# Two of eight normaliser chunks of a linear-attention layer routed through memory instead of through TensorE

## Chip, cores and metric

The kernel runs on one core of one Trainium2 chip. The metric is the device time of one execution in microseconds (us), as the median of several executions. The engines are called by the names of the profile: PE is TensorE's matmul, PEld its weight load, DVE VectorE, ACT ScalarE, POOL GpSimd, and SP SyncE, which here only issues transfers and waits (SPq in the rows).

## What is computed

The input x has 8 batches of 512 tokens with 128 features. The first half is a linear attention with 16 heads of 64 features, the second a mixture of eight experts of which each token takes two. The part that matters, cut from the reference:

```python
q, k, v = split(x @ W_qkv)                       # 16 heads of 64
q, k = relu(q @ W_f + b_f), relu(k @ W_f + b_f)
kv = einsum('bhnd,bhne->bhde', k, v)
out = einsum('bhnd,bhde->bhne', q, kv)
normalizer = einsum('bhnd,bhd->bhn', q, k.sum(axis=2))
out = out / (normalizer[..., None] + 1e-06)
x = layernorm(x + out @ W_out + b_out)
# then: x = layernorm(x + mixture_of_experts(x))
```

There is one normaliser for each head and token. It has to divide all 64 features of its head.

## The kernel before

**Layout.** The 1024 query features lie as eight chunks of 128 partitions (`q_act[:, c, :]`, features down the partitions, the 512 tokens of a batch along a row). One chunk holds two heads, 64 partitions each. The reciprocal normalisers of a batch are a tile `rn[:, 1, :]` in which the two heads of chunk c stand on two neighbouring partitions of 128. To multiply chunk c by them, each of the two rows has to be brought to 64 partitions.

**How it is brought there before.** `r_hi`, `r_rest` (ACT, two ACTIVATEs, lines 838 and 839) and `r_hl` (DVE, line 1196) split the reciprocals into a high and a low part. For each chunk `spread_norm(c)` (line 566) is one PE matmul of a constant matrix of ones and zeros with `r_hl`, into one of the two halves of the PSUM tile `psG`. `normalise(c)` (line 1124) is the DVE product of `q_act` and `psG` into `qn`, and `output(c)` (line 575) the PE matmul of `qn` with the mixed values, summed over c in `psO`.

**Order of the work.** The orders of all engines are written out by hand, with semaphores between them. `attention(b)` is called for b = 0 to 8. Call b works on the keys and queries of batch b (`cur`, b below 8) and on the output of batch p = b - 1 (`prev`, b above 0). On PE a call is: `keys(0)`, `keys(1)`, `spread_norm(0)`; then for c = 0 to 7 `keys(c + 1)` (three matmuls, lines 465 to 467), `spread_norm(c + 1)`, `turn_keys(c)` (four transposes, line 554) and `output(c - 1)`; then `output(7)`, the eight `queries`, the logits of batch p, the normaliser sums (`norms`, line 597), the Gram matrices (`gram`, lines 465 to 467) and `mix` (line 622). In call 8 only `spread_norm` and `output` are left.

**The loop over c on the other engines.** ACT evicts each key chunk (`key`, into `kT`) and splits its transpose (`key_hi`, into `k_hi`). DVE does, for each c, `normalise(c)`, `key_lo(c - 1)` (line 893, into `k_lo`) and, for odd c, a row sum over two chunks (line 1136). `turn_keys(c)` waits for the eviction of chunk c and for `key_lo(c - 2)`; `output(c)` waits for `normalise(c)`; `spread_norm(c)` waits for `normalise(c - 2)`. In call 7 the DVE also works out a table of expert blocks in five parts (`early_table`), one in each of the steps c = 1 to 5. In calls 1 to 7 one or two expert weights are split by ACT and DVE as well (`SPLIT_AT`), and SP stores each and loads the next (lines 330 to 334).

**Where the reciprocals come from.** Late in call b the DVE adds the epsilon to the sums (line 1187) and takes two reciprocals of half a batch each (line 1191), after which the count of `n_step` is 3 (b + 1). `spread_norm(0)` of call b + 1 is the first that needs them.

**SP's queue before.** After the loads of the start, SP goes through the eight experts (wait for the split, store, load), then waits for the last batch's tokens and loads the second expert layer's weights (line 337), and later feeds the expert stage, which takes the time from some 303 us on.

Of the kernel before, what the change touches and what calls it, by code (L numbers as in the profile page):

```python
# [19 lines left out]
ALU = mybir.AluOpType  # L20
ACT = mybir.ActivationFunctionType
AX_X = mybir.AxisListType.X
F32 = mybir.dt.float32
# [6 lines left out]
P = 128  # L30
D = 128
B, S = 8, 512
N = B * S
TILES = S // P
H, DH = 16, 64
HD = H * DH
CH = HD // P
E, F = 8, 512
# [7 lines left out]
EARLY = -(-(SAFE * S * TOPK - E * (BLK - 1)) // BLK)  # L46
LATE = NBLK - EARLY
ERAS = (4, SAFE, B - 1, B)
# [9 lines left out]
CHAIN_AT = {37: ((0, 4),), 40: ((4, 6), (6, 7))}  # L58
NORM_AT = {38: 0}
PAIRED = 8  # L60
ROW = D + 4
XS_ROWS = E * REGION + BLK
NOWHERE = E * REGION
# [7 lines left out]
SPLIT_AT = {1: ((0, 2), (1, 5)), **{b: ((b, 3),) for b in range(2, B)}}  # L71
# [10 lines left out]
QUAD = 32  # L82
# [32 lines left out]
def program(nc, x, xT, wqkvT, wf, bf, wout, bout, gwT, w12, consts, out):  # L115
    ctx = ExitStack()
    with ctx:
        def sb(name, shape, dt=F32):
            return ctx.enter_context(nc.sbuf_tensor(name, shape, dt))

        def pb(name, shape, dt=F32):
            return ctx.enter_context(nc.psum_tensor(name, shape, dt))

        def sem(name):
            return ctx.enter_context(nc.semaphore(name))


        wb = nc.dram_tensor("expert_weights", [E, P, W_ROW], F32, kind="Internal").ap()
        xs = nc.dram_tensor("expert_rows", [XS_ROWS, ROW], F32, kind="Internal").ap()
        ys = nc.dram_tensor("expert_results", [TOPK * N, D], F32, kind="Internal").ap()  # L130


# [2 lines left out]
        def con(name, rows=P):  # L135
# [14 lines left out]
        q_act = sb("q_act", [P, CH, S])  # L150
        gm = sb("gm", [P, HD])
        mixed = sb("mixed", [P, CH, D])
        kT = sb("kT", [P, KT_SLOTS, S])
        ksum = sb("ksum", [P, CH])
        qn = sb("qn", [P, 4, S])
        rows_2 = [sb(f"rows{i}", [P, TILES, TOPK, ROW]) for i in range(2)]
        zeros = sb("zeros", [P, BLK // P, ROW])
        warm = sb("warm", [P, 2])
# [6 lines left out]
        tri_b = sb("tri_b", [P, P], BF16)  # L165
        ksd = sb("ksd", [P, CH, QUAD])
        rn = sb("rn", [P, 2, S])
        r_hi, r_rest = sb("r_hi", [P, S], F32R), sb("r_rest", [P, S])
        spread = sb("spread", [P, CH, P], F32R)
        r_hl = sb("r_hl", [P, S], F32R)  # L170
# [25 lines left out]
        at_row = sb("at_row", [1, len(ERAS) * E])  # L196
        jump = sb("jump", [1, len(ERAS) * E])
        endi = sb("endi", [1, E], I32)
        past = [sb(f"past{i}", [1, LATE * len(ERAS) * E]) for i in range(2)]
        tab = sb("tab", [1, 3, NBLK])  # L200
        tabi = sb("tabi", [1, 2, NBLK], I32)

# [3 lines left out]
        woutd = x1[:, 0:2 * CH, :].rearrange("p (c a) d -> p c a d", a=2)  # L206
        zT = qn[:, 3, :]
        kT_space = kT[:, :, :].rearrange("p c s -> p (c s)")
        rn_space = rn[:, :, :].rearrange("p a s -> p (a s)")
        qn_space = qn[:, :, :].rearrange("p a s -> p (a s)")  # L210
        hT = [q_space[:, v * FC * BLK:(v + 1) * FC * BLK].rearrange("p (c s) -> p c s", c=FC) for v in range(2)]
        yrow = [q_space[:, 2 * FC * BLK + 2 * u * D:2 * FC * BLK + 2 * (u + 1) * D].rearrange("p (c d) -> p c d", d=D) for u in range(SLOTS)]
        xrow = [space[:, 2 * u * ROW:2 * (u + 1) * ROW].rearrange("p (c d) -> p c d", d=ROW)
                for space, fit in ((kT_space, 7), (rn_space, ROW_SLOTS - 7)) for u in range(fit)]
# [10 lines left out]
        psG = pb("psG", [P, 2, 512])  # L225
# [10 lines left out]
        def bank_of(n):  # L236
            return n % 2 if n >= PAIRED else 0

        def before(n):
            return n if n <= PAIRED else n - 1  # L240

# [11 lines left out]
        ksum_done, ks_done, n_pe, n_step, qn_done, o_pe, zT_done = (  # L253
            sem(n) for n in ("ksum_done", "ks_done", "n_pe", "n_step", "qn_done", "o_pe", "zT_done"))
# [9 lines left out]
        w1_out = [sem(f"w1_out{i}") for i in range(2)]  # L264
        wb_in, w2_in = sem("wb_in"), sem("w2_in")
        in_xr0, in_fold_q, in_fold_v, tab_step = (sem(n) for n in ("in_xr0", "in_fold_q", "in_fold_v", "tab_step"))
        r_h, r_l, bc_pe, in_spread, spread_ready = (sem(n) for n in ("r_h", "r_l", "bc_pe", "in_spread", "spread_ready"))
        warmed, ends, padded, filled_rows = sem("warmed"), sem("ends"), sem("padded"), sem("filled_rows")
        scattered_2 = [sem(f"scattered_{i}") for i in range(2)]
# [6 lines left out]
        N_STEPS, LN_STEPS, ST_STEPS, ROUTE_STEPS = 3, 12, 2 * TILES, 22  # L276
# [26 lines left out]
        def _(sp):  # L303
# [19 lines left out]
            def load_w1(ex):  # L323
                sp.dma_start(w1_raw[ex % 2], w12[ex, :, 0:F]).then_inc(in_w1[ex % 2], 16)
# [2 lines left out]
            sp.dma_start(wb[:, :, 2 * F + FC:], w12[:, :, F + FC + FC * D:]).then_inc(wb_in, 16)  # L327
            load_w1(0)
            load_w1(1)
            for ex in range(E):  # L330
                sp.wait_ge(w1_l, ex + 1)
                sp.dma_start(wb[ex, :, 0:2 * F], w1_split[ex % 2].bitcast(F32)).then_inc(w1_out[ex % 2], 16)
                if ex + 2 < E:
                    load_w1(ex + 2)
            sp.wait_ge(x_l, B)
            sp.wait_ge(x_h, B)
            sp.dma_start(w2_all.rearrange("p (e n) -> p e n", e=E), w12[:, :, F + FC:F + FC + FC * D].rearrange("e p n -> p e n")).then_inc(w2_in, 16)
# [122 lines left out]
        def _(pe):  # L460
# [25 lines left out]
            def gate_mean():  # L486

                pe.wait_ge(in_c, 16)
                pe.wait_ge(in_small, 32)
                mm(psS[:, 0:E], con("ones"), gw[:, :], start=True, stop=True).then_inc(mean_pe, 1)  # L490
# [35 lines left out]
            def attention(b):  # L526
                cur, prev = b < B, 1 <= b <= B
                p = b - 1

                def keys(c):  # L530
                    if c == 0:
                        pe.wait_ge(xT_l, b + 1)
                    if c >= 2:
                        pe.wait_ge(kT_done, CH * b + c - 1)
                    if b == 0 and c % 4 == 0:
                        pe.wait_ge(fold_lo, 1 + c // 4)
                    at = slice(c * P, (c + 1) * P)
                    three(bankA[c % 2], wk_hi[:, at], wk_lo[:, at], xT_hi[:, :], xT_lo[:, :]).then_inc(kT_pe, 1)

                def turn_keys(c):  # L540
                    pe.wait_ge(kT_done, CH * b + c + 1)
                    if c == 0 and prev:
                        pe.wait_ge(m_first, b)
                    if c == 0 and b == 0:
                        pe.wait_ge(in_ident, 16)
                    if c == 1 and prev:
                        pe.wait_ge(m_second, b)
                    if c == 1 and b == 0:
                        pe.wait_ge(fold_lo, 2)
                    if c >= 2:  # L550
                        pe.wait_ge(k_l, CH * b + c - 1)
                    for t in range(TILES):
                        at = slice(t * P, (t + 1) * P)
                        last = pe.transpose(bankA[2 + c % 2][:, at], kT[:, (CH * b + c) % KT_SLOTS, at], con("ident"))  # L554
                    last.then_inc(kr_pe, 1)

                def spread_norm(c):

                    if c == 0:
                        pe.wait_ge(r_l, p + 1)  # L560
                        pe.wait_ge(spread_ready, 1)
                    if c < 2:
                        pe.wait_ge(g_done, 2 * (p + 1))
                    else:
                        pe.wait_ge(qn_done, CH * p + c - 1)
                    mm(psG[:, c % 2, :], spread[:, c, :], r_hl[:, :], start=True, stop=True).then_inc(bc_pe, 1)  # L566
# [64 lines left out]
                for c in range(CH):  # L631
                    if cur and c and c + 1 < CH:
                        keys(c + 1)
                    if prev and c + 1 < CH:
                        spread_norm(c + 1)
                    if cur:
                        turn_keys(c)
                    if b == 0 and c == 2:
                        fold_queries()
                    if b == 0 and c == 3:  # L640
                        gate_mean()
                    if prev and c:
                        output(c - 1)
# [247 lines left out]
        def _(dve):  # L891
# [71 lines left out]

            def gone(cum, n, k):

                table_ = past[0][:, 0:n * k].rearrange("p (n k) -> p n k", k=k)
                tb(dve.tensor_tensor(table_, cum[:, None, 16:16 + k].broadcast_to([1, n, k]),
                                     con("block", 1)[:, 0:n, None].broadcast_to([1, n, k]), ALU.is_le))
                tb.wait()

            def summed(to, by, n, k):

                table_, scaled = (past[i][:, 0:n * k].rearrange("p (n k) -> p n k", k=k) for i in range(2))
                tb(dve.tensor_tensor(scaled, table_, by[:, None, 0:k].broadcast_to([1, n, k]), ALU.mult))
                tb.wait()
                tb(dve.tensor_reduce(tab[:, to, 0:n], scaled, AX_X, ALU.add))
                tb.wait()
# [136 lines left out]
            def attention(b):  # L1114
                cur, prev = b < B, 1 <= b <= B
                p = b - 1
                router = Router(p)

                def normalise(c):

                    dve.wait_ge(bc_pe, CH * p + c + 1)
                    if c >= 4:
                        dve.wait_ge(o_pe, CH * p + c - 3)
                    dve.tensor_tensor(qn[:, c % 4, :], q_act[:, c, :], psG[:, c % 2, :], ALU.mult).then_inc(qn_done, 1)  # L1124

                def key_lo(c):
                    dve.wait_ge(k_h, CH * b + c + 1)
# [138 lines left out]
            for t in range(2, TILES):  # L1266
                i = (B - 1) * TILES + t
# [29 lines left out]
```

## Time and profile before

| what | us |
|---|---|
| median of 3 runs | 463.35 |
| lowest and highest run | 462.35, 464.86 |
| the profiled execution, its own time | 462.59 |
| its span, first to last instruction | 460.8 |

The span is 1.79 us shorter than the execution's own time. PE is busy for 429.2 us of the span (93%), PEld 342.2 us, DVE 325.5 us (71%), ACT 274.4 us (60%) and POOL 162.3 us (35%). Matmuls are pipelined, and the profile draws each longer than the slot that it takes: the time that a matmul costs is read from one start to the next. In a timeline a row has its start, its length, the engine, the line, the output and its inputs, the shape, how many instructions it merges, and in brackets how long the engine stood idle before it and what ended that.

### The profile page before, as it was taken

What the parts mean: (1) busy time and instruction counts of PE and PEld (TensorE: products, weight loads), DVE (VectorE), ACT (ScalarE), POOL (GpSimd) and SP (SyncE); (2) the same over time, 40 slices, a digit from 0 to 9 for tenths busy, and PEclk for the clock granted to TensorE, in tenths of its full rate; (3) what the DMA queues carried; (4) which work ended last, traced back from release to release, by engine and by line L of the source; (5) the groups of instructions that cost most, each with busy time, mean ns of one, the idle gap of its engine ahead of it and who ended that gap; (6) DMA issues with size and microseconds to landing.
All of it is one profiled execution on the core that took longest, in us unless ns stands there. A gap on an engine that the chain in (4) does not pass through costs nothing.

```text
span 460.8 us, 8851 instructions
## 1 busy us (share of the span) xinstructions
PE 429.2 (93%) x2784; PEld 342.2 (74%) x2784; DVE 325.5 (71%) x946; ACT 274.4 (60%) x538; POOL 162.3 (35%) x164
## 2 busy tenths in 40 slices
PE   6989999999999999999999979889999999999940
PEld 5876776776776776776776647569999999999840
DVE  3574968969968968969968997755874433456786
ACT  2664766756756756756656636339555565555565
POOL 2011101431431431431431402425777655555550
PEclk9899999999999999999999999999999999999985
DMA  8980220210210210210100060499696899499534
GB/s 221 303 213 0 71 68 1 74 43 2 69 43 6 70 41 7 68 43 7 60 29 7 24 230 24 142 310 297 192 245 217 280 359 302 130 355 329 165 125 137
DMA packets 40013, 61.16 MB, mean 133 GB/s; under 512 B 6287, under 2 KB 27284, under 8 KB 39840
## 3 DMA queue, kind: packets, MB, share of 16 engines
q1 hardware_dynamic: 30560, 49.65, 34.4%
q0 software_dynamic: 4544, 8.54, 5.3%
q10 hardware_dynamic: 4864, 2.42, 1.8%
q8 instruction: 23, 0.38, 0.3%
q14 instruction: 22, 0.18, 0.1%
HBM read 44.55 MB, written 17.49 MB: 135 GB/s over the span
## 4 chain that ended last, share of the span: by engine, by line
PE 77%; DVE 11%; issue 3%; DMA 3%; ACT 2%; ACTq 1%; POOL 1%; SPq 1%; POOLq 0%; DVEq 0%
PE psO L575 11%; PE psA L465 9%; PE psA L466 9%; PE psA L467 9%; PE psG L705 7%; PE psA L554 6%; PE psS L705 4%; PE psG L465 3%; PE psA L622 3%; PE psG L566 3%; PE psG L466 3%; PE psG L467 3%; PE psG L597 2%; PE psS L511 1%; DMA rn<-expert_rows 1%
## 5 line engine op out<-in xcount | busy, mean ns | idle before, releaser
L425 POOL DMA_INDIRECT expert_rows<-rows,pos x64 | 62.1, 970 | 95.9 <-PE psA L467 67.0
L450 POOL DMA_INDIRECT expert_results<-q_act,kT x56 | 55.4, 989 | 44.5 <-DVE q_act L1213 33.5
L726 ACT ACTIVATE kT<-psA,bf_col 128x512 f32<-128x512 f32 x64 | 44.0, 688 | 37.9 <-PE psA L467 37.5
L575 PE MATMUL psO<-qn,mixed 128*128 128x512 f32 x128 | 64.0, 593 | 0.0
L726 ACT ACTIVATE q_act<-psA,bf_col 128x512 f32<-128x512 f32 x64 | 44.1, 689 | 25.9 <-PE psA L467 25.3
L893 DVE TENSOR_TENSOR k_lo<-psA,k_hi 128x512 fp32r<-128x512 f32 x64 | 43.9, 686 | 7.0 <-ACT k_hi L726 6.3
L1124 DVE TENSOR_TENSOR qn<-q_act,psG 128x512 f32<-128x512 f32 x64 | 42.9, 680 | 8.2 <-PE psG L566 8.2
L705 PE MATMUL psG<-x_raw,q_act 128*128 x384 | 46.9, 275 | 0.3 <-ACT q_act L867 0.2
L705 PEld LDWEIGHTS psG<-x_raw,q_act 128*128 128x128 f32 x384 | 44.9, 192 | 0.7 <-issue 0.7
L554 PEld LDWEIGHTS psA<-cst,kT 128*128 128x128 f32 x256 | 32.0, 142 | 17.4 <-issue 5.8
L465 PE MATMUL psA<-xT_hi,wk_hi 128*128 128x512 f32 x64 | 41.5, 649 | 2.8 <-POOL xT_lo L416 2.8
L726 ACT ACTIVATE k_hi<-psA 128x512 fp32r<-128x512 f32 x64 | 38.3, 598 | 9.6 <-PE psA L554 9.5
L554 PE MATMUL psA<-cst,kT 128*128 128x128 f32 x256 | 39.5, 277 | 4.1 <-DVE k_lo L893 2.3
L1136 DVE TENSOR_REDUCE ksum<-kT 128x2 f32<-128x1024 f32 x32 | 38.7, 1208 | 0.0
L416 POOL TENSOR_TENSOR x_lo<-x_raw,x_hi 128x512 fp32r<-128x512 f32 x8 | 10.3, 1293 | 68.5 <-ACT x_hi L726 68.5
L416 POOL TENSOR_TENSOR xT_lo<-xT_raw,xT_hi 128x512 fp32r<-128x512 f32 x8 | 10.2, 1281 | 63.3 <-ACT xT_hi L726 63.3
L705 PE MATMUL psS<-x_raw,q_act 128*128 x240 | 29.2, 275 | 0.0
L465 PE MATMUL psA<-xT_hi,wq_hi 128*128 128x512 f32 x64 | 28.8, 450 | 0.0
L726 ACT ACTIVATE xT_hi<-psG 128x256 fp32r<-128x256 f32 x24 | 9.3, 387 | 32.2 <-PE psG L675 32.2
L705 PEld LDWEIGHTS psS<-x_raw,q_act 128*128 128x128 f32 x240 | 28.0, 192 | 0.0
L566 PE MATMUL psG<-r_hl,spread 128*128 128x512 f32 x64 | 26.4, 433 | 1.4 <-DVE r_hl L1196 0.7
L867 ACT ACTIVATE q_act<-psA,k_lo 128x256 f32<-128x256 f32 x60 | 23.6, 478 | 6.0 <-PE psA L467 5.8
(199 smaller groups left out, 1044.0 us busy)
## 6 DMA issues: line engine op xcount, KB each, us to landing
k_hi<-expert_weights SPq DMA_DIRECT2D x15, 578.0 KB
k_lo<-expert_weights SPq DMA_DIRECT2D x15, 578.0 KB, 5.4
w_more<-expert_weights SPq DMA_DIRECT2D x9, 578.0 KB, 4.7
expert_weights<-w_more SPq DMA_DIRECT2D x8, 512.0 KB, 2.9
kT<-expert_rows SPq DMA_DIRECT2D x28, 132.0 KB, 4.5
w_raw<-w SPq DMA_DIRECT2D x8, 256.0 KB, 3.4
x_raw<-w SPq DMA_DIRECT2D x1, 2048.0 KB, 9.2
x<-expert_results SPq DMA_DIRECT2D x4, 512.0 KB, 6.3
```

The source lines that it names most:

```text
L425: pool.indirect_dma_start(xs, bass.IndirectOffsetOnAxis(ap=pos_2[o % 2][:, j, k:k + 1], axis=0), rows_2[o % 2][:, j, k, :], None).then_inc ...
L450: pool.indirect_dma_start(ys, bass.IndirectOffsetOnAxis(ap=xrow[r][:, c, D:D + 1].bitcast(I32), axis=0), yrow[u][:, c, :], None, bounds_ch ...
L465: mm(outp, a_hi, b_hi, start=start, stop=False)
L466: mm(outp, a_hi, b_lo, start=False, stop=False)
L467: return mm(outp, a_lo, b_hi, start=False, stop=stop)
L554: last = pe.transpose(bankA[2 + c % 2][:, at], kT[:, (CH * b + c) % KT_SLOTS, at], con("ident"))
L566: mm(psG[:, c % 2, :], spread[:, c, :], r_hl[:, :], start=True, stop=True).then_inc(bc_pe, 1)
L575: mm(psO[:, :], mixed[:, c, :], qn[:, c % 4, :], start=c == 0, stop=c == CH - 1).then_inc(o_pe, 1)
L705: last = mm(psY2[bank_of(n)][:, t, :], hT[v][:, c, t * P:(t + 1) * P], w2_all[:, ds(expert * (FC * D) + c * D, D)], start=c == 0, stop=c = ...
L726: return act.activation(out_, in_, func, **kw)
L893: return dve.tensor_tensor(out_, full_, hi_.bitcast(F32), ALU.subtract)
L1124: dve.tensor_tensor(qn[:, c % 4, :], q_act[:, c, :], psG[:, c % 2, :], ALU.mult).then_inc(qn_done, 1)
```

## The change

- Chunks 6 and 7 (`RELAYED` = 6 and up) are no longer spread by PE in calls 1 to 7: 14 of the 64 `spread_norm` matmuls go. Call 8 keeps all eight.
- At the end of each of the calls 0 to 6, SP waits until both reciprocals are done, and then issues four transfers. Two store the two rows of chunk 6 and of chunk 7 into a tensor in device memory, `rs[i]`, each row written 8 times (16 rows of 2 KB, 32 KB). Then SP waits for each store and loads it into `bc[:, i, :]`, 128 partitions of 2 KB (256 KB), each of the 16 rows read by 8 partitions.
- `normalise(6)` and `normalise(7)` wait for their load instead of for PE, and read `bc`, in SBUF, instead of `psG`, in PSUM.
- SP's loop over the experts is cut up by batch, so that the waits for the reciprocals stand between the stores and loads of the experts that belong to their calls.
- To make room, the scratch rows `past` of the block tables are made shorter. The late table, which is worked out in the expert stage, uses the first partition of `gm` and `mixed` in their place.

```diff
+RELAYED = 6
+COPIES = 8
...
+        rs = nc.dram_tensor("normalisers", [CH - RELAYED, 2, COPIES, S], F32, kind="Internal").ap()
...
+        bc = sb("bc", [P, CH - RELAYED, S])
...
-            for ex in range(E):
+
+            def keep_split(ex):
                 sp.wait_ge(w1_l, ex + 1)
                 sp.dma_start(wb[ex, :, 0:2 * F], w1_split[ex % 2].bitcast(F32)).then_inc(w1_out[ex % 2], 16)
                 if ex + 2 < E:
                     load_w1(ex + 2)
+
+            for b in range(B):
+                for ex, _ in SPLIT_AT.get(b, ()):
+                    keep_split(ex)
+                if b < B - 1:
+                    sp.wait_ge(n_step, N_STEPS * (b + 1))
+                    for i in range(CH - RELAYED):
+                        row = (i + RELAYED) % 4 * QUAD + 2 * (i + RELAYED)
+                        sp.dma_start(rs[i], rn[row:row + 2, 1, None, :].broadcast_to([2, COPIES, S])).then_inc(r_out[i], 16)
+                    for i in range(CH - RELAYED):
+                        sp.wait_ge(r_out[i], 16 * (b + 1))
+                        sp.dma_start(bc[:, i, :], rs[i][:, :, None, :].broadcast_to([2, COPIES, DH // COPIES, S])).then_inc(bc_in[i], 16)
...
-                    if prev and c + 1 < CH:
+                    if prev and c + 1 < (RELAYED if cur else CH):
                         spread_norm(c + 1)
...
-                    dve.wait_ge(bc_pe, CH * p + c + 1)
+                    relayed = cur and c >= RELAYED
+                    if relayed:
+                        dve.wait_ge(bc_in[c - RELAYED], 16 * (p + 1))
+                    else:
+                        dve.wait_ge(bc_pe, RELAYED * p + c + 1)
                     if c >= 4:
                         dve.wait_ge(o_pe, CH * p + c - 3)
-                    dve.tensor_tensor(qn[:, c % 4, :], q_act[:, c, :], psG[:, c % 2, :], ALU.mult).then_inc(qn_done, 1)
+                    dve.tensor_tensor(qn[:, c % 4, :], q_act[:, c, :], bc[:, c - RELAYED, :] if relayed else psG[:, c % 2, :], ALU.mult).then_inc(qn_done, 1)
```

## Rows read from the trace of the kernel before

**Rows 1.** Busy time by stretch: call 4, then call 7 of `attention`.

```profile
core 0: us, PE busy (x) PEld busy (x) DVE busy (x) ACT busy (x) POOL busy (x), PEclk, DMA share, GB/s
...
148.60:183.10 34.50, 34.50 (x195) 24.48 (x193) 28.00 (x76) 22.35 (x39) 10.28 (x10) 1.00 0.12 40
...
252.30:289.00 36.70, 33.92 (x169) 22.64 (x165) 31.53 (x87) 20.62 (x35) 9.30 (x9) 1.00 0.25 87
```

**Rows 2.** Timeline of call 4, steps c = 5 to 7, PE, PEld and ACT.

```profile
160.57 0.40 PE L566 MATMUL psG<-r_hl,spread 128*128 128x512 f32 x1
...
160.81 0.60 PE L554 MATMUL psA<-cst,kT 128*128 128x128 f32 x4
...
162.80 0.39 PE L566 MATMUL psG<-r_hl,spread 128*128 128x512 f32 x1
...
163.00 0.69 ACT L726 ACTIVATE kT<-psA,bf_col 128x512 f32<-128x512 f32 x1 [0.96 <-PE psA L467]
163.03 0.60 PE L554 MATMUL psA<-cst,kT 128*128 128x128 f32 x4
...
163.47 1.02 PE L575 MATMUL psO<-qn,mixed 128*128 128x512 f32 x2
...
163.90 0.14 PEld L554 LDWEIGHTS psA<-cst,kT 128*128 128x128 f32 x1 [0.24 <-ACT kT L726]
...
164.33 0.60 PE L554 MATMUL psA<-cst,kT 128*128 128x128 f32 x4
...
164.76 1.88 PE L575 MATMUL psO<-qn,mixed 128*128 128x512 f32 x4
```

**Rows 3.** Line 566 in calls 1 to 6: the group, and who waited for it.

```profile
L566 PE MATMUL psG<-r_hl,spread x48: 391/392/402, 46.0 to 232.3; 128*128 128x512 f32 x48
...
  DVE qn L1124: 5.6, 11
```

**Rows 4.** Timeline of DVE in the same steps of call 4 as rows 2.

```profile
161.58 0.68 DVE L1124 TENSOR_TENSOR qn<-q_act,psG 128x512 f32<-128x512 f32 x1
...
162.17 0.68 DVE L893 TENSOR_TENSOR k_lo<-psA,k_hi 128x512 fp32r<-128x512 f32 x1
...
163.23 0.69 DVE L1124 TENSOR_TENSOR qn<-q_act,psG 128x512 f32<-128x512 f32 x1 [0.38 <-PE psG L566]
```

**Rows 5.** Timeline of DVE, call 4: a product with both operands in SBUF; the reciprocals.

```profile
158.34 0.68 DVE L893 TENSOR_TENSOR w_more<-w_raw,w_more 128x512 fp32r<-128x512 f32 x1
...
177.52 3.37 DVE L1191 RECIPROCAL rn<-rn 128x256 f32<-128x256 f32 x2
```

**Rows 6.** Timeline of call 5: SP's store of an expert, and `normalise(6)`.

```profile
193.60 0.34 SPq L332 DMA_DIRECT2D expert_weights<-w_more  x1
...
196.12 0.68 DVE L1124 TENSOR_TENSOR qn<-q_act,psG 128x512 f32<-128x512 f32 x1
```

**Rows 7.** DMA issues: out<-in, queue, count, KB each, median us from issue to landing.

```profile
expert_weights<-w_more SPq DMA_DIRECT2D x8, 512.0 KB, 2.9
...
w_raw<-w SPq DMA_DIRECT2D x8, 256.0 KB, 3.4
x_raw<-w SPq DMA_DIRECT2D x1, 2048.0 KB, 9.2
...
expert_rows<-zeros SPq DMA_DIRECT2D x9, 132.0 KB, 18.1
```

**Rows 8.** Timeline of call 7, DVE from the second part of the loop on.

```profile
268.46 1.21 DVE L1136 TENSOR_REDUCE ksum<-kT 128x2 f32<-128x1024 f32 x1
269.58 0.42 DVE L974 TENSOR_TENSOR past<-past,jump 1x272 f32<-1x272 f32 x1
...
270.92 0.67 DVE L1124 TENSOR_TENSOR qn<-q_act,psG 128x512 f32<-128x512 f32 x1
271.51 0.67 DVE L893 TENSOR_TENSOR k_lo<-psA,k_hi 128x512 fp32r<-128x512 f32 x1
```

**Rows 9.** Timeline of call 7, PE: `turn_keys(7)`.

```profile
272.33 0.63 PE L554 MATMUL psA<-cst,kT 128*128 128x128 f32 x4 [2.16 <-DVE k_lo L893]
```

More of the change, by code:

```diff
@@ L198, in program @@
         endi = sb("endi", [1, E], I32)
-        past = [sb(f"past{i}", [1, LATE * len(ERAS) * E]) for i in range(2)]
+        past = [sb(f"past{i}", [1, EARLY * 2 * E]) for i in range(2)]
         tab = sb("tab", [1, 3, NBLK])
@@ L208, in program @@
         kT_space = kT[:, :, :].rearrange("p c s -> p (c s)")
+        late_past = [gm[0:1, :], mixed[:, :, :].rearrange("p c d -> p (c d)")[0:1, :]]
         rn_space = rn[:, :, :].rearrange("p a s -> p (a s)")
@@ L266, in program @@
         in_xr0, in_fold_q, in_fold_v, tab_step = (sem(n) for n in ("in_xr0", "in_fold_q", "in_fold_v", "tab_step"))
+        r_out, bc_in = ([sem(f"{n}{c}") for c in range(CH - RELAYED)] for n in ("r_out", "bc_in"))
         r_h, r_l, bc_pe, in_spread, spread_ready = (sem(n) for n in ("r_h", "r_l", "bc_pe", "in_spread", "spread_ready"))
@@ L964, in gone @@
             def gone(cum, n, k):
-                table_ = past[0][:, 0:n * k].rearrange("p (n k) -> p n k", k=k)
+                table_ = (past if n == EARLY else late_past)[0][:, 0:n * k].rearrange("p (n k) -> p n k", k=k)
                 tb(dve.tensor_tensor(table_, cum[:, None, 16:16 + k].broadcast_to([1, n, k]),
@@ L971, in summed @@
             def summed(to, by, n, k):
-                table_, scaled = (past[i][:, 0:n * k].rearrange("p (n k) -> p n k", k=k) for i in range(2))
+                table_, scaled = ((past if n == EARLY else late_past)[i][:, 0:n * k].rearrange("p (n k) -> p n k", k=k) for i in range(2))
                 tb(dve.tensor_tensor(scaled, table_, by[:, None, 0:k].broadcast_to([1, n, k]), ALU.mult))
```

## The prediction, made before the change was run

> **What bounds the kernel now.** I read the busy time by stretch first, then the timeline of one call, then who waited for whom. In call 4 PE is busy for 34.50 of 34.50 us at a granted clock of 1.00, while DVE is busy for 28.00 and the transfers use 0.12 of the engines' time [rows 1]. A busy PE need not be at its peak, so the timeline has to show that one matmul starts where the last one's slot ends. It does: through steps 5 to 7 PE goes from spreading to turning keys to output with no gap that another engine ends [rows 2]. Calls 1 to 6 look alike; from `normalise(6)` of call 4 [rows 4] to that of call 5 [rows 6] it is 34.54 us. So there time is won by taking work off PE. Call 7 is different: the stretch is longer, PE is busy for 33.92 of 36.70 us [rows 1], and `turn_keys(7)` comes after 2.16 us in which PE stood idle until `key_lo` was done [rows 9]. There DVE sets the end of the loop.
>
> **What is removed.** Each `spread_norm` is drawn 0.39 us long [rows 3], but its slot is start to start: 160.57 to 160.81 and 162.80 to 163.03 [rows 2], 0.24 and 0.23 us. Two go in each call of 1 to 7. In calls 1 to 6 that is 12 x 0.235 = 2.8 us.
>
> **Does what follows close up?** The tightest place is `turn_keys(7)`. Reckon from the end of `keys(7)`'s slot, 162.80, where the removed matmul starts [rows 2]. PE then has turning 163.03 to 163.47 (0.44) and output 163.47 to 164.33 (0.86), and could start `turn_keys(7)` 1.30 us after `keys(7)`. It needs the eviction of chunk 7, which ACT ends at 163.69; the weight load that waited for it began at 163.90 and takes 0.14. This is 1.10 + 0.14 = 1.24 us after `keys(7)`: ready with 0.06 us to spare. It also needs `key_lo(5)`, which ended at 162.85 [rows 4], while the new start is 164.33 - 0.47 = 163.86: 1.0 us to spare. `output(6)` then starts at 164.76 - 0.47 = 164.29 and needs `normalise(6)`, done at 162.26; `output(7)` starts 0.86 later, at 165.15, and needs `normalise(7)`, which stood idle 0.38 us for the removed matmul [rows 4] and now needn't. So I take the whole of both slots; the bound below is one slot of the two, should ACT slip by a quarter of a microsecond.
>
> **Call 7** gains nothing. From the row sum at 268.46 DVE goes on without a gap through the table, `normalise(6)` at 270.92 and `key_lo(5)` at 271.51 [rows 8], which is what PE waits for [rows 9]. Two matmuls less on PE lengthen that wait by the same. From below this is 0, from above 2 x 0.235 = 0.5 us; I take 0. Call 8 keeps its eight matmuls.
>
> **DVE's product from SBUF.** `normalise` from PSUM takes 0.68 us [rows 4], and a DVE product of the same size with both operands in SBUF takes 0.68 us as well [rows 5]. Cost: 0. DVE waited 5.6 us for line 566 in calls 1 to 6, 11 times [rows 3]; part of this goes, but DVE is not the bound there, so it pays nothing.
>
> **The relay.** SP's four transfers wait for the reciprocals, whose end in call 4 is 177.52 + 3.37 = 180.89 [rows 5]. `normalise(6)` of call 5 begins at 196.12 [rows 6]. That is 15.2 us. An issue on SP takes about 0.4 us (0.34 in [rows 6]). The store is 32 KB; the nearest store of the trace, 512 KB, lands in 2.9 us. The load is 256 KB into 128 partitions; the trace's own load of that size and form lands in 3.4 us [rows 7]. First copy: 0.4 + 0.4 + 2.9 + 0.4 + 3.4 = 7.5 us after the reciprocals, the second 0.4 to 1 us later. Both are there by 189.5 and the first is hidden by 7 us. SP's other work stays in place: the expert's store in call 5 is issued at 193.60 [rows 6], when DVE has made the split, and SP is past its relay by 185.5. What stands behind SP's new waits is then only such an issue, and nobody waits soon for it. The bytes (0.58 MB in each call) fall where the engines are at 0.12. The cover of the relay is the Gram matrices, mixing and six steps of the loop; if it were gone the price is that of the second rival.
>
> **The late table** uses other memory for the same instructions, after `gm` and `mixed` have been read for the last time: 0. The expert stage comes behind a chain of PE work and moves forward as one.
>
> **Sum.** The profiled execution took 462.59 us: 462.59 - 2.8 = 459.8, with a span of 458.0. The median of the runs is 0.76 us above that execution: 463.35 - 2.8 = 460.55. About 0.5%, or 2.3 us, is what a measurement of this kernel can tell from no change, so the gain is only just beyond it.
>
> **Rival one: a wait takes the slot's place.** The 0.06 us to spare at `turn_keys(7)` is narrow, and it rests on ACT's eviction following `keys(7)` at once. If ACT or a semaphore is later by one slot, one matmul of each call is won and the other turns into a wait: 6 x 0.235 = 1.4 us, which gives 461.95. For it speaks that PE's weight load there already waits for ACT [rows 2]; against it, that no matmul waited.
>
> **Rival two, slower: the copies arrive late.** `normalise(7)` must start by about 165.15 - 0.7 - 0.1 = 164.35 in call 4's time, or 198.9 in call 5: 18.0 us after the reciprocals. That is the point from which it decides, and beyond it each microsecond costs one in each call, since PE stands before `output(7)`. A load that only a few transfer engines carry would do it. The row of 2048 KB took 9.2 us [rows 7], eight times the bytes of one copy. Were one copy as slow as that, and the second queued behind it, they would land at 180.9 + 4.1 + 9.2 = 194.2 and at 203.4, so 4.5 us late in six calls: + 27.0 - 2.8 = + 24.2, or 487.5. Call 7 would have about the time it needs. The zeros' 132 KB even took 18.1 us [rows 7], a median of nine from the start and the expert stage. Against all this stands that both nearest rows landed in 2.9 and 3.4 us in these very calls. The Trainium skill ("DMA: Bandwidth & Descriptors", why a DMA increments its semaphore by 16) says that a transfer is divided along the outermost dimension that isn't 1 on either side, over at most 16 engines and by a count that divides both sizes. By it the stores, with two partitions outermost, go by two engines, and the loads by two as well unless the source's 2 and 8, which lie one behind the other in memory, are joined to 16; I take them as joined, since they are contiguous. If they are not, this rival is the case, and no run here shows it yet.
>
> **Rival three: it doesn't show.** The matmuls go as reckoned, but the time is won back elsewhere: the expert stage holds waits for stores and loads of its own, and if one of them hangs on something that the attention doesn't move, some or all of the 2.8 us turns into a wait there: 463.35 at most. Against it: every transfer of that stage is issued after attention's last semaphores.
>
> **How the numbers follow.** Forecast, both slots won in six calls: 0.72. Rival one 0.10, rival three 0.08, rival two 0.08, and 0.02 for more than the forecast (call 7 gains too, 460.0). Runs of this kernel lie 1.0 below to 1.5 above their median. With a gain of 2.8 against a bound of 2.3 about one in six of the forecast's cases is measured within 0.5%, which leaves 0.60 there and 0.02 from the last case: faster 0.62. Within 0.5%: 0.12 and the first and third rival, 0.30. Slower 0.08. The range goes from 459.0, call 7's gain and 1 us of spread below, to 463.0, which takes in rival one and most of rival three.
>
> **What would show it.** In calls 1 to 6 of the changed profile: 0.47 us less in each period (34.1), six of line 566 where eight were, the turning of keys right behind the last key matmul in steps 5 and 6, `turn_keys(7)` 1.30 us after `keys(7)` with no wait, `normalise(6)` and `(7)` of 0.68 us with no wait for a transfer, and landings of the copies below 4 us each. In call 7 PE's waits for `key_lo` in steps 5 to 7 should grow by 0.47 us together. The prediction is wrong if DVE waits for a load of `bc`, if PE shows a new gap in step 7, or if the expert stage is longer than before.

## The result, and the profile after

| | before | after |
|---|---|---|
| median of 20 runs each, us | 462.14 | 460.04 |
| profiled execution: own time | 462.59 | 461.07 |
| profiled execution: span | 460.8 | 459.2 |

The ratio of after to before is 0.9951, with a 95% interval of 0.9931 to 0.9971: 2.3 us faster, between 1.3 and 3.2. (The front of this document gives 463.35 for the kernel before, from three runs; beside the changed kernel it was run again.) One execution of it took 940.39 us there, and one of an experiment 2443.77 us; neither is in a ratio. The forecast of 2.8 us lies in the interval, and 460.5 is close to the median. But the two profiled spans differ by 1.6 us only, so the first question is where the other 1.2 us of the forecast are.

A good mark in the timeline is `mix`, which PE does at the end of each call. The start of its first matmul, calls 0, 6 and 7, in the timeline of the kernel before:

```profile
42.66 1.97 PE L622 MATMUL psA<-vo,gm 128*64 128x128 f32 x32
...
250.77 1.97 PE L622 MATMUL psA<-vo,gm 128*64 128x128 f32 x32
...
289.28 1.97 PE L622 MATMUL psA<-vo,gm 128*64 128x128 f32 x32
```

and of the kernel after, where the line has become 641:

```profile
42.26 1.97 PE L641 MATMUL psA<-vo,gm 128*64 128x128 f32 x32
...
247.64 1.97 PE L641 MATMUL psA<-vo,gm 128*64 128x128 f32 x32
...
287.78 1.97 PE L641 MATMUL psA<-vo,gm 128*64 128x128 f32 x32
```

Differences of these starts, and of the last to the span, split the change of the span into four parts:

| stretch | before | after | change |
|---|---|---|---|
| start, to `mix` of call 0 | 42.66 | 42.26 | -0.40 |
| calls 1 to 6 | 208.11 | 205.38 | -2.73 |
| call 7 | 38.51 | 40.14 | +1.63 |
| from there to the end | 171.52 | 171.42 | -0.10 |

**Calls 1 to 6** did what was forecast: 2.73 us. Four of them went from 34.54 or 34.55 to 34.06 or 34.07. In calls 2 and 5 (34.93 and 34.99 before, 34.55 and 34.56 after) PE also waits 0.2 to 0.3 us for the epsilon step in front of the second Gram matrix, in both kernels.

PE in steps 5 to 7 of call 4 of the kernel after, to be read against [rows 2]:

```profile
158.59 0.39 PE L486 MATMUL psA<-xT_hi,wk_lo 128*128 128x512 f32 x1
158.82 0.60 PE L573 MATMUL psA<-cst,kT 128*128 128x128 f32 x4
159.25 1.02 PE L594 MATMUL psO<-qn,mixed 128*128 128x512 f32 x2
...
160.57 0.39 PE L486 MATMUL psA<-xT_hi,wk_lo 128*128 128x512 f32 x1
160.81 0.60 PE L573 MATMUL psA<-cst,kT 128*128 128x128 f32 x4
161.24 1.02 PE L594 MATMUL psO<-qn,mixed 128*128 128x512 f32 x2
162.10 0.60 PE L573 MATMUL psA<-cst,kT 128*128 128x128 f32 x4
162.54 1.88 PE L594 MATMUL psO<-qn,mixed 128*128 128x512 f32 x4
```

The turning of keys (line 573) follows the last key matmul by one slot, 0.23 and 0.24 us, where a spreading matmul stood between them. `turn_keys(7)` at 162.10 comes 1.29 us behind that of step 6 at 160.81, that is 0.43 + 0.86, with no wait. Its first weight load, which waits for the eviction of chunk 7, came earlier than forecast:

```profile
161.74 0.14 PEld L573 LDWEIGHTS psA<-cst,kT 128*128 128x128 f32 x1 [0.31 <-ACT kT L745]
```

It ends at 161.88, 0.22 us ahead of the turning, where the prediction had 0.06 us to spare.

The products of chunks 6 and 7 on DVE, with `bc` as second operand, answer to [rows 4]; the reciprocals before them answer to [rows 5]:

```profile
159.83 0.68 DVE L1147 TENSOR_TENSOR qn<-q_act,bc 128x512 f32<-128x512 f32 x1
...
161.03 0.68 DVE L1147 TENSOR_TENSOR qn<-q_act,bc 128x512 f32<-128x512 f32 x1
...
175.30 3.37 DVE L1214 RECIPROCAL rn<-rn 128x256 f32<-128x256 f32 x2
...
193.90 0.68 DVE L1147 TENSOR_TENSOR qn<-q_act,bc 128x512 f32<-128x512 f32 x1
```

They take 0.68 us and wait for nothing. The relay between them, first SP's issues in the timeline:

```profile
178.69 1.36 SPq L350 DMA_DIRECT2D normalisers<-rn  x2
181.64 1.80 SPq L353 DMA_DIRECT2D bc<-normalisers  x2
```

and the loads' row among the DMA issues (count, KB each, median us to landing):

```profile
bc<-normalisers SPq DMA_DIRECT2D x14, 256.0 KB, 3.3
```

The reciprocals end at 178.67, the loads are issued from 181.64 on and land 3.3 us later: the second, issued at 182.89, is there by 186.2, over 7 us before `normalise(6)` at 193.90. One issue takes 0.66 us for a store and 0.55 us for a load instead of the 0.4 I reckoned (the 1.80 us of the row also hold 0.7 us in which SP waits for the second store), on a queue that has nothing else to do.

**Call 7** is the surprise. PE in steps 5 to 7 and in the first queries, kernel after, to be read against [rows 9]:

```profile
262.83 0.63 PE L573 MATMUL psA<-cst,kT 128*128 128x128 f32 x4 [0.80 <-ACT kT L745]
...
265.56 0.63 PE L573 MATMUL psA<-cst,kT 128*128 128x128 f32 x4 [0.53 <-DVE k_lo L912]
266.02 1.02 PE L594 MATMUL psO<-qn,mixed 128*128 128x512 f32 x2
269.21 0.63 PE L573 MATMUL psA<-cst,kT 128*128 128x128 f32 x4 [2.16 <-DVE k_lo L912]
269.67 2.80 PE L594 MATMUL psO<-qn,mixed 128*128 128x512 f32 x4
271.48 1.41 PE L484 MATMUL psA<-xT_hi,wq_hi 128*128 128x512 f32 x1
272.69 0.63 PE L485 MATMUL psA<-xT_lo,wq_hi 128*128 128x512 f32 x1
273.12 0.63 PE L486 MATMUL psA<-xT_hi,wq_lo 128*128 128x512 f32 x1
```

The same two waits of steps 5 and 6 in the kernel before:

```profile
265.96 0.63 PE L554 MATMUL psA<-cst,kT 128*128 128x128 f32 x4 [0.19 <-ACT kT L726]
...
268.69 0.63 PE L554 MATMUL psA<-cst,kT 128*128 128x128 f32 x4 [0.19 <-DVE k_lo L893]
```

The last wait is 2.16 us as before. The two removed slots turned up as longer waits in steps 5 and 6 (0.80 and 0.53 us; before, both were 0.19): the turnings still lie 2.73 and 3.65 us apart, before 2.73 and 3.64, as PE doesn't set the pace of this loop. After the wait, though, everything is slower: four output matmuls are drawn 2.80 us long instead of 1.88, and the first query matmuls follow at 0.43 us instead of 0.23. The busy time of four microseconds around and behind the end of the wait says why. Columns as in [rows 1]; first the kernel before, then after:

```profile
272.00:276.00 4.00, 3.67 (x15) 2.47 (x16) 4.00 (x7) 1.18 (x2) 0.34 (x1) 1.00 0.95 358
```

```profile
270.00:274.00 4.00, 4.00 (x9) 2.22 (x8) 3.06 (x5) 0.68 (x2) 0.00 (x0) 0.57 0.71 268
```

The granted clock is 1.00 before and 0.57 after: PE ran at its lower level, 1.2 GHz, for most of these 4 us, and did 9 matmuls. The kernel before did 15 in its window, which still holds 0.33 us of the wait, and 16 in one that lies as far behind the wait as the other's (273.12 to 277.12). Four microseconds at 0.57 lose about 4 x 0.43 = 1.7 us, by an estimate from this row, and that is the 1.63 us.

### The profile page after: what moved, and what is told of

It reads as the page before. It is cut to its first block, busy times and chain, and to the rows that moved or that the text cites. A ratio compares the mean times of both kernels' runs of the same rounds, so it can differ in the third digit from the quotient of the medians.

```text
span 459.2 us, 8851 instructions
## 1 busy us (share of the span) xinstructions
PE 426.5 (93%) x2770; PEld 339.9 (74%) x2770; DVE 324.5 (71%) x946; ACT 273.2 (59%) x538; POOL 162.8 (35%) x164
## 4 chain that ended last, share of the span: by engine, by line
PE 79%; DVE 11%; issue 3%; DMA 2%; ACT 2%; ACTq 1%; SPq 1%; POOL 1%; POOLq 0%; DVEq 0%
PE psO L594 12%; PE psA L484 10%; PE psA L485 9%; PE psA L486 9%; PE psG L724 7%; PE psA L573 6%; PE psS L724 4%; PE psG L484 3%; PE psA L641 3%; PE psG L485 3%; PE psG L486 3%; PE psG L585 2%; PE psG L616 2%; PE psS L530 1%; PE psG L694 1%
## 5 line engine op out<-in xcount | busy, mean ns | idle before, releaser
L1147 DVE TENSOR_TENSOR qn<-q_act,psG 128x512 f32<-128x512 f32 x50 | 33.4, 682 | 6.3 <-PE psG L585 6.3
L484 PE MATMUL psG<-k_hi,x_hi 128*128 128x512 f32 x64 | 26.6, 416 | 0.6 <-DVE rn L1210 0.6
```

What stands on the lines that cost most here:

```text
L484: mm(outp, a_hi, b_hi, start=start, stop=False)
L1147: dve.tensor_tensor(qn[:, c % 4, :], q_act[:, c, :], bc[:, c - RELAYED, :] if relayed else psG[:, c % 2, :], ALU.mult).then_inc(qn_done, 1)
```

## The experiments

The twelve runs were made in three groups, each on one chip, beside the kernel before. The first group is the changed kernel once more, the relay in calls 1 to 6, the relay in call 7 alone, and the changed kernel with the stretch filled. The second is the relay beside all matmuls, one copy, three chunks, and the kernel before with the stretch filled. The third is the rest. The medians of the kernel before were 463.08 us in the first group, 484.19 in the second and 484.49 in the third (see the last section), so only ratios are compared across groups. In each trace I read call 7 from `mix` to `mix`, and calls 1 to 6 in the same way.

| kernel | ratio, interval | calls 1 to 6, us | call 7, us |
|---|---|---|---|
| changed, once more | 0.9952, 0.9925 to 0.9979 | 205.35 | 40.20 |
| relay in calls 1 to 6 | 0.9907, 0.9878 to 0.9936 | 205.33 | 40.20 |
| the same, once more | 0.9956, 0.9926 to 0.9986 | 205.37 | 38.50 |
| relay in call 7 alone | 0.9990, 0.9965 to 1.0015 | 208.07 | 40.18 |
| changed, stretch filled | 0.9922, 0.9898 to 0.9947 | 205.38 | 38.52 |
| relay, and all matmuls | 1.0024, 0.9998 to 1.0050 | 208.11 | 40.18 |
| one copy | 0.9945, 0.9923 to 0.9967 | 205.33 | 40.18 |
| three chunks, calls 1 to 6 | 0.9930, 0.9897 to 0.9964 | 204.09 | 38.49 |
| before, stretch filled | 0.9988, 0.9960 to 1.0015 | 208.08 | 38.49 |
| three chunks, filled | 0.9874, 0.9857 to 0.9892 | 204.07 | 38.50 |
| before, once more | 1.0007, 0.9984 to 1.0031 | 208.14 | 38.50 |
| before, for its trace alone | - | 208.03 | 38.49 |

### The changed kernel once more

> The changed kernel once more, beside the three below. My theory: attention calls 1 to 6 are each 0.47 us shorter (2.8 in all), and in call 7 PE stands idle longer before the last turning of keys, after which its granted clock falls to 0.5 for some 2.5 us, in some executions; that costs 1.6 us there when it happens. Expected: 460.0, between 457 and 462.5, with a wider spread of the runs than the kernel before. Rival (the gain is lost evenly over the calls, or in the expert stage): the same time, but with call 7 at 38.5 us from mix to mix and the loss elsewhere.

Ratio 0.9952, as the first time. Calls 1 to 6 take 205.35 us and call 7 40.20, with the clock down again: the loss is in call 7 alone, and the rival is out. The wider spread of runs that was expected didn't come: 3.8 us, where the kernel before had 5.8.

### Relay in calls 1 to 6 alone

```diff
+RELAY_CALLS = tuple(range(1, B - 1))
...
-                if b < B - 1:
+                if b + 1 in RELAY_CALLS:
...
-                    if prev and c + 1 < (RELAYED if cur else CH):
+                    if prev and c + 1 < (RELAYED if b in RELAY_CALLS else CH):
```

> Relay in calls 1 to 6 alone; call 7 has its eight spreading matmuls on PE as before. My theory: the whole 2.8 us of the six calls stays and the fall of the clock in call 7 becomes as rare as in the kernel before: 459.3 against 462.1 before, call 7 38.5 us from mix to mix with a granted clock of 1.00 throughout. Rival, the fall has nothing to do with the two matmuls: as the changed kernel, 460.0, with the fall in call 7 as often.

The gain of the six calls stands (205.33). But call 7 takes 40.20 us with all its eight spreading matmuls in place. PE behind the wait, in this kernel:

```profile
265.23 0.63 PE L574 MATMUL psA<-cst,kT 128*128 128x128 f32 x4 [0.19 <-DVE k_lo L913]
...
268.88 1.04 PE L574 MATMUL psA<-cst,kT 128*128 128x128 f32 x4 [2.16 <-DVE k_lo L913]
269.71 3.20 PE L595 MATMUL psO<-qn,mixed 128*128 128x512 f32 x4
```

and the busy time of the three microseconds behind it, columns as in [rows 1]:

```profile
269.00:272.00 3.00, 3.00 (x7) 1.73 (x7) 2.65 (x4) 0.60 (x1) 0.00 (x0) 0.50 1.03 399
```

The waits are those of the kernel before, 0.19 and 2.16 us, and yet the clock went to 0.50. So the two removed matmuls are not needed for the fall; my first theory, that they cause it, fell here. The same kernel in the third group, below, had no fall. The ratio of this run, 0.9907 from six executions, is better than the slots explain: 0.994 lies outside its interval. Of the repetition it was 0.9956.

### Relay in call 7 alone

```diff
-RELAY_CALLS = tuple(range(1, B - 1))
+RELAY_CALLS = tuple((B - 1,))
```

> Relay in call 7 alone. My theory: nothing is won, since DVE sets the end of that loop, and where the clock falls 1.6 us are lost: 462.1 to 463.7, ratio to before 1.000 to 1.004. Rival, call 7 gains what the others gain: 0.5 us less than before.

Calls 1 to 6 are those of the kernel before (208.07), call 7 has the fall (40.18). The time is the same within 0.25%: removing matmuls where DVE sets the pace wins nothing. That it should lose 1.6 us against a kernel that never falls isn't borne out by the ratio (0.9990, at most 1.0015). Either the kernel before falls in some executions too, or this one doesn't in most of its own; one trace of it can't tell, and the three traces of the kernel before show no fall.

### The idle stretch filled, in the changed kernel

```diff
                     if prev and c:
                         output(c - 1)
+                    if b == B - 1 and c == 6:
+                        for _ in range(9):
+                            mm(psG[:, 0, :], spread[:, 6, :], r_hl[:, :], start=True, stop=True)
```

> The changed kernel with nine matmuls more, that nobody reads, between the output matmul and the last turning of keys in call 7, 9 x 0.235 = 2.1 us into an idle stretch of 2.16 us. My theory, the idle stretch brings the clock down: it stays at 1.00, call 7 is 38.5 us, and the time is 459.3 with a spread as narrow as that of the kernel before. Rival, the clock falls for another reason (the transfers at that time, or at random): the fall stays, 460.0 or up to 0.3 us more for the matmuls that reach past the stretch.

PE in this kernel, and below it the busy time of the stretch that follows:

```profile
267.82 2.65 PE L666 MATMUL psG<-r_hl,spread 128*128 128x512 f32 x9
270.54 0.63 PE L574 MATMUL psA<-cst,kT 128*128 128x128 f32 x4
271.00 1.88 PE L595 MATMUL psO<-qn,mixed 128*128 128x512 f32 x4
```

```profile
270.00:274.00 4.00, 3.93 (x17) 2.34 (x16) 4.00 (x7) 0.97 (x2) 0.13 (x1) 1.00 0.98 366
```

The nine matmuls lie in the stretch, the turning of keys comes when `key_lo` is done as before, and the clock stays at 1.00: 38.52 us. The transfers of that moment are as dense as ever (0.98, and 0.95 in the kernel before, which had no fall either), so dense transfers alone don't bring the clock down. The ratio went from 0.9952 to 0.9922, about 1.4 us, though the two intervals overlap, and the medians of the two kernels, 460.36 and 459.46 us, differ by 0.9. This is one trace, and the kernel before escapes with its stretch unfilled: that filling keeps the clock up is likely by the ratio, and not shown.

### The relay beside all eight matmuls

```diff
-                    if prev and c + 1 < (RELAYED if cur else CH):
+                    if prev and c + 1 < CH:
...
-                        dve.wait_ge(bc_pe, RELAYED * p + c + 1)
+                        dve.wait_ge(bc_pe, CH * p + c + 1)
```

> The changed kernel with all eight spreading matmuls kept on PE in every call; the products of chunks 6 and 7 still wait for the relay and read bc, and nobody reads the two matmuls. It holds the relay's own cost alone. My theory, the relay is hidden and the gain is PE's slots and nothing else: as the kernel before, calls 1 to 6 at 34.5 to 34.9 us from mix to mix, ratio to before 0.998 to 1.002. Rival (the gain comes from DVE's earlier products, or the relay disturbs): calls shorter than 34.5, or longer than before.

Calls 1 to 6 take 208.11 us, to 0.01 us what they took before. The relay and the products from `bc` cost nothing and win nothing; the gain is PE's slots. The clock fell in call 7 here with the matmuls kept, which is all that speaks for a loss in the ratio of 1.0024, just outside the 0.998 to 1.002 expected.

### One copy in place of eight

```diff
-COPIES = 8
+COPIES = 1
```

> The changed kernel with COPIES = 1: each row is written once and read by 64 partitions, so the source of a load has two rows outermost in place of sixteen. My theory (the division of a transfer follows its outermost dimension, here 2): a load lands in 9 us or more instead of 3.3, the two one after the other, normalise(7) waits for bc in calls 1 to 6, and the time is 470 to 490. Rival, the copies aren't needed: landing 3 to 4 us, calls at 34.1, 460.

Half of the theory held. First the timeline, SP's issue of the loads and the product that needs them; then the busy time by stretch, of which the last two columns matter, the share of the transfer engines and GB/s:

```profile
179.69 1.05 SPq L354 DMA_DIRECT2D bc<-normalisers  x2
...
193.69 0.68 DVE L1148 TENSOR_TENSOR qn<-q_act,bc 128x512 f32<-128x512 f32 x1
```

```profile
182.00:186.00 4.00, 4.00 (x21) 3.00 (x20) 3.31 (x6) 3.22 (x6) 2.56 (x3) 1.00 0.13 51
...
190.00:192.00 2.00, 2.00 (x11) 1.34 (x10) 1.78 (x4) 1.49 (x3) 0.00 (x0) 1.00 0.13 49
```

A share of 0.13 is two engines of sixteen, at some 25 GB/s each. That is what the Trainium skill's rule says for two rows outermost ("DMA: Bandwidth & Descriptors", why a DMA increments its semaphore by 16), and the trace agrees. With eight copies a load landed in 3.3 us, and the engines' share, in the kernel of the forecast, is more than two engines can give:

```profile
182.50:184.50 2.00, 2.00 (x14) 1.63 (x13) 1.58 (x3) 1.97 (x5) 1.29 (x1) 1.00 0.50 153
```

That fits a 2 and an 8 that are joined, as the prediction took them. But the price was wrong. At 50 GB/s the 512 KB of both loads take about 10.5 us in all, and the share is still 0.13 up to 192. `normalise(6)` begins at 193.69 with no wait. Calls 1 to 6 are 205.33, the ratio 0.9945: the copies buy some 6 us of slack that nobody needs.

### Three chunks relayed

```diff
-RELAYED = 6
+RELAYED = 5
...
-        past = [sb(f"past{i}", [1, EARLY * 2 * E]) for i in range(2)]
+        past = [full[:, :, :].rearrange("p r e -> p (r e)"), sb("past1", [1, EARLY * 2 * E])]
```

and relay in calls 1 to 6 alone, as above.

> Relay of chunks 5 to 7 in calls 1 to 6 alone (the scratch row of the early table shares its place with another to make room). My theory, PE is still the bound with three slots less: calls 1 to 6 lose 0.7 us each against before, 33.8 us, 4.2 in all, 1.4 less than with two chunks: ratio to before 0.988 to 0.992. Rival, DVE or ACT becomes the bound: calls at 34.0 and no gain over two chunks.

Calls 1 to 6 take 204.09 us, 4.0 less than before and 1.25 less than with two chunks; the four plain calls are 33.86 us against 34.55, three slots of 0.23 us, as reckoned. PE is still the bound. The ratio, 0.9930, is outside the 0.988 to 0.992 expected, but its interval reaches down to 0.9897. There was no fall in this trace.

### The idle stretch filled, in the kernel before

```diff
+                    if b == B - 1 and c == 6:
+                        for _ in range(9):
+                            mm(psS[:, :], spread[:, 6, :], r_hl[:, :], start=True, stop=True)
```

> The kernel before, with nine matmuls more that nobody reads in the idle stretch of call 7. The fall of the clock came with all eight spreading matmuls in call 7 as well, so my first theory of it has fallen. New theory: the idle stretch of 2.16 us, which both kernels have, brings it down in most executions of either, and the profiled execution of before was one of the few that escaped. Then this kernel gains about as much over before as the filled changed kernel over the changed one, 1 to 1.6 us: ratio 0.9965 to 0.998, call 7 at 38.5. Rival, the kernel before hardly ever falls: ratio 1.000.

Inconclusive by its time: 0.9988 lies between the two theories and the interval holds 1. Call 7 was 38.49, with no fall.

### Both together, and three traces more

> Relay of chunks 5 to 7 in calls 1 to 6 alone, and nine unread matmuls in the idle stretch of call 7. The two gains are of different places and should add up: 6 x 0.7 = 4.2 us from the slots, and the clock at 1.00 in call 7, which is 38.5 us long in every execution: ratio to before 0.987 to 0.991. Rival, the filled stretch is worth nothing beside the kernel before, which seldom falls: 0.991.

> The kernel before, unchanged, for its trace and as a control of the comparison: ratio 1.000. The open question is how often its clock falls in call 7. So far the stretch from mix to mix was 40.2 us, with the clock down, in all four traces in which the two matmuls were gone from call 7, and in two of the four in which they were kept. Theory: with the two matmuls kept it falls in some executions only, so of this trace and the next two one or two show 38.5. Rival, it falls as often as without them and the first two escapes were luck: all three show 40.2.

> The kernel before once more, for its trace alone: 38.5 us in call 7 with the clock at 1.00, or 40.2 with its fall, as said for the run ahead of it.

> Relay in calls 1 to 6 alone once more: in call 7 it is the kernel before. Calls 1 to 6 at 34.07 us, call 7 at 38.5 or 40.2 as said for the run of the kernel before. Ratio to before 0.994 (the slots alone, 2.8 us), where the first measurement said 0.9907 with six runs.

Three chunks with the stretch filled is the fastest kernel of the case: 0.9874, 1.1 to 1.4% below the kernel before, on a chip where that took 484.49. Its slots are worth 4.1 us (0.9916 of 484), which lies outside the interval, 0.9857 to 0.9892; an avoided fall would add at most 1.65 us (0.988). But in call 7 this kernel is the kernel before with its stretch filled, and no unfilled kernel fell on this chip in three traces. So where the rest comes from is open; the median is of only four executions.

The two traces of the kernel before and the repetition of the relay in calls 1 to 6 all show 38.5 us. Neither theory foresaw this: one expected one or two of them to fall, the other all three. Over the whole case, call 7 of the unfilled kernels:

| in call 7 | traces | with a fall |
|---|---|---|
| the two matmuls gone from PE | 4 | 4 |
| the two matmuls kept | 7 | 2 |
| the stretch filled | 3 | 0 |

Were the six falls dealt out among the eleven unfilled traces by chance, all four of the first kind would be among them in 1 of 22 cases. That leans to the removed matmuls making the fall likelier, and doesn't show it. The three filled traces say less still: three traces picked by chance would all be among the eight without a fall in 1 of 6.5 cases.

The same traces can be sorted in other ways, which no run tells apart. By the relay, the kernels whose call 7 was fed by it fell in five traces of five, the others in one of six. By chip, the unfilled kernels fell in one trace of two in the profiled pair, in three of three in the first group, in two of three in the second and in none of three in the third. And by the moment: the fall doesn't come at a fixed distance behind the wait. In the relay in calls 1 to 6 the clock is at 0.50 from 269.00 on, 0.12 us behind it. In the changed kernel, whose wait ends at 269.21, it begins near 270.5, 1.3 us behind, by this stretch:

```profile
270.00:271.00 1.00, 1.00 (x3) 0.52 (x2) 1.00 (x2) 0.47 (x1) 0.00 (x0) 0.75 1.04 406
```

So whether the clock falls behind the same wait may depend on the moment at which the wait comes, and the starts of the traces differ by microseconds. No run held the moment fixed; by this reading the three filled traces may only have been lucky.

## Why the prediction was right, and where not

**The slots.** Forecast 12 x 0.235 = 2.8 us in calls 1 to 6, measured 2.73 in the profiled pair and 2.73 to 2.78 in the five other traces with two chunks relayed and removed there. The relay beside all matmuls left these calls unchanged, so nothing else adds to the gain. Reading a matmul's cost from start to start, not from its drawn 0.39 us, was what made the size right.

**What closes up.** `turn_keys(7)` came 1.29 us after that of step 6, with no wait, and with 0.22 us to spare instead of 0.06: the prediction added the weight load's start as it stood in the old order, 0.21 us behind the eviction's end, where it now came 0.05 us behind. Rival one, a wait in the slot's place, didn't happen in any trace, not even with three chunks gone.

**The relay.** Forecast there after 8.6 us and hidden by 7; measured there after 7.5 and hidden by over 7. A store took 0.66 us to issue and a load 0.55, about one and a half times what I said; on an idle queue it made no odds.

**DVE from SBUF.** 0.68 us forecast and measured.

**Rival two, the slower side.** Its condition, a load on few engines, was built with one copy and is real; its price was not. I gave each of the two loads the 9.2 us that a transfer of 2048 KB took [rows 7]. Two engines moved 25 GB/s each, so one load takes about 5 us and both together 10.5; with the stores they were there 13.5 us after the reciprocals (178.46 to 192), inside the 15.2 us. So rival two is not slower even where its condition is met.

**Rival three, won back in the expert stage.** It didn't happen: the stretch from the last `mix` to the end took 171.52 us before and 171.42 after. The reason given against it was not exact, though. The 2048 KB of the second expert layer's weights, for one, are issued inside attention, in call 7, at 267.82 before and 264.70 after.

**Call 7: the step that failed.** "Call 7 gains nothing ... I take 0", between 0 and a gain of 0.5. The idle time grew and the end of the loop stayed where DVE put it, as said, but I bounded the cost at nothing for a longer idle PE. In the profiled execution the clock then fell and cost 1.63 us. The rows showed a stall of 2.16 us, and a clock of 1.00 over the whole call, in one execution; the prediction has no term for the clock at all. The fall isn't a property of the change alone: it came in two traces in which call 7 had all its spreading matmuls, in one of them with call 7 wholly as before. What sets it off, and whether the changed kernel has it more often, stays open. No filled trace had it (none of three), which is too few to show that filling prevents it. The sign that the prediction gave, waits for `key_lo` longer by 0.47 us together, came out as 0.95 us more in the brackets of steps 5 and 6, one of them a wait for ACT: part of the old idle time had stood ahead of the spreading matmuls.

**The number.** 460.5 forecast, 460.04 measured beside 462.14 for the kernel before, which is 1.2 lower than the median I started from. A ratio is the fairer comparison: 2.8 of 463.35 is 0.9940, measured 0.9951 and 0.9952. The missing tenth of a per cent would be 0.5 us, a third of a fall; that is arithmetic, not shown. That 460.5 and 460.04 lie so close is in part luck: from 462.14 the forecast gives 459.3, and the measured median is 0.7 us above that. The gain, 0.49%, also falls on the line of 0.5% that the prediction drew between its 0.62 and its 0.30.

## What to carry to other kernels

Where one engine's instructions follow each other slot by slot, work taken off it is won nearly in full (2.73 of 2.8 us), and its price is the distance between starts; ask in each stage, not once for the kernel, which engine that is. Where it is not the bound, taking work off PE buys idle time and nothing else, and behind idle time of PE the clock may be down: look at the granted clock behind every wait of a microsecond or two, and in more than one execution. A detour through memory of two hops and 7.5 us is free when the consumer is 15 us away; here one of 13.5 us was free as well.

## What was not expected of the hardware

**Behind the same two microseconds of idle PE its clock fell, or didn't.** The last wait was 2.15 or 2.16 us in the eleven unfilled traces. In six of them PE went to the lower level behind it, which made call 7 1.6 to 1.7 us longer, and in five it stayed at 1.00.

**Chips differ in one stage alone.** The kernel before took 463.08 us on the first group's chip and 484.19 and 484.49 on the two others. Calls 1 to 6 are the same to 0.1 us (208.11 and 208.14). The difference lies behind attention: from the last `mix` to the end it is 171.5 us in the profiled execution of the front and 192.5 in one of the same kernel on the third group's chip. The first 47 us of the expert stage, in these two executions:

```profile
303.00:350.00 47.00, 45.62 (x396) 44.97 (x397) 30.71 (x121) 30.26 (x74) 26.27 (x27) 1.00 0.86 263
```

```profile
303.00:350.00 47.00, 39.39 (x319) 37.85 (x320) 26.75 (x108) 25.39 (x61) 21.81 (x21) 0.96 0.78 235
```

There PE did 319 matmuls against 396. Up to 320 us the two are level (139 and 138 matmuls), and from there to 350 it is 183 against 260. Why is open; no run was made for it.

**The start moves more than the change.** `mix` of call 0 began anywhere from 41.00 to 44.54 us in these traces, a range of 3.5 us against a gain of 2.7. A change of half a per cent can't be read from two spans; it can be read from the distances inside them.
